# Mixture-of-experts tiles in groups of four, with the narrow down products on two row groups of TensorE

## The reference, cut to what matters

```python
gu = jnp.einsum('th,efh->tef', x, w_gate_up)      # 64 experts, 2 * 176 rows each
g, u = (gu[..., :FFN], gu[..., FFN:])
act = jax.nn.silu(g) * u
act = act * comb[:, :, None]                      # the token's share of expert e
routed = jnp.einsum('tef,ehf->th', act, w_down)   # 176 -> 256
shared = jnp.einsum('tf,hf->th', jax.nn.silu(sg) * su, ws_down)
return routed + shared
```

## Time and profile before

| | |
|---|---|
| median of 3 runs | 294.2 us (292.29 to 294.91) |
| profiled execution | 293.05 us, span 291.2 us |
| TensorE busy | 258.4 us, 89% |
| POOL busy | 178.2 us, 61% |
| DVE busy | 150.3 us, 52% |
| ACT busy | 126.2 us, 43% |
| DMA | 89.08 MB, mean 306 GB/s |

### The profile page before, as it was taken

One profiled execution on the slowest core, in us unless ns is written; L12 is line 12 of the kernel. 1 busy time (PEld: TensorE's weight loads), 2 busy tenths in 40 slices (PEclk: granted clock), 3 DMA queues, 4 the chain that ended last, 5 costly groups with the idle time before them and its releaser, 6 DMA issues.

```text
span 291.2 us, 6600 instructions
## 1 busy us (share of the span) xinstructions
PE 258.4 (89%) x1674; PEld 225.5 (77%) x1674; DVE 150.3 (52%) x696; ACT 126.2 (43%) x374; POOL 178.2 (61%) x155
## 2 busy tenths in 40 slices
PE   6998758888889879999999999999999999999810
PEld 4695436666656669999999999999999999999700
DVE  3834897799996744544433333333333333334355
ACT  2524433332322544555555555555555555555300
POOL 9301257767776734677877667776766665577600
PEclk9999997799999999999999999999999999999995
DMA  6999999999943638999999999999999999988597
GB/s 162 393 429 430 417 361 377 390 399 387 382 173 134 202 85 198 334 327 352 351 353 333 332 321 325 330 325 321 327 323 329 332 332 334 335 184 161 77 322 260
DMA packets 50632, 89.08 MB, mean 306 GB/s; under 512 B 6578, under 2 KB 37379, under 8 KB 49571
## 3 DMA queue, kind: packets, MB, share of 16 engines
q1 hardware_dynamic: 29714, 63.75, 60.9%
q0 software_dynamic: 12816, 17.12, 27.6%
q10 hardware_dynamic: 8064, 7.80, 7.9%
HBM read 58.11 MB, written 30.54 MB: 304 GB/s over the span
## 4 chain that ended last, share of the span: by engine, by line
PE 66%; DVE 17%; DMA 7%; issue 4%; POOL 3%; ACT 2%; SPq 0%; POOLq 0%; DVEq 0%; ACTq 0%
PE PS L1188 29%; PE PS L1200 10%; PE PS L1201 10%; PE PS L1057 5%; PE PS L1140 3%; DVE M L888 2%; DMA VXG<-x_slots 2%; DMA XN<-acc 2%; DVE X L979 2%; POOL x_slots L449 2%; PE PS L1020 2%; DMA acc<-PT,IDR 2%; PE PS L1014 1%; PE PS L1027 1%; PE PS L1035 1%
## 5 line engine op out<-in xcount | busy, mean ns | idle before, releaser
L1188 PEld LDWEIGHTS PS<-XT,WA 128*128 128x128 f32 (+1 forms) x852 | 105.5, 187 | 5.0 <-ACT XNT L556 0.8
L1188 PE MATMUL PS<-XT,WA 128*128 128x128 f32 (+1 forms) x852 | 106.0, 274 | 1.0 <-ACT XNT L556 0.6
L492 POOL DMA_INDIRECT acc<-PT,IDR x52 | 81.0, 1558 | 37.5 <-ACT PT L660 17.3
L934 DVE TENSOR_TENSOR AC<-SG,PS 128x128 f32<-128x128 f32 x71 | 20.4, 288 | 95.6 <-ACT SG L628 95.2
L660 ACT ACTIVATE PT<-PS,WT 128x256 f32<-128x256 f32 x70 | 33.1, 473 | 34.4 <-PE PS L1201 33.7
L446 POOL DMA_INDIRECT x_slots<-HX,SLOT x36 | 35.1, 976 | 16.0 <-issue 9.6
L1200 PE MATMUL PS<-WA,AC 128*128 128x256 f32 x140 | 41.8, 381 | 0.0
L1201 PE MATMUL PS<-WB,AC 128*128 128x256 f32 x140 | 41.7, 379 | 0.0
L492 POOL DMA_INDIRECT out_rows<-PT,IDR x18 | 28.1, 1561 | 14.9 <-ACT PT L660 6.9
L549 ACT COPY XT<-PS 128x256 f32<-128x256 f32 x73 | 27.1, 372 | 19.8 <-PE PS L1057 17.4
L627 ACT ACTIVATE SG<-PS 128x128 f32<-128x128 f32 x71 | 19.7, 277 | 27.8 <-PE PS L1188 27.8
(11 more groups left out here) (154 smaller groups left out, 310.1 us busy)
## 6 DMA issues: line engine op xcount, KB each, us to landing
WA<-in_wa SPq DMA_DIRECT2D x71, 496.0 KB, 13.7
x_slots<-WA SPq DMA_DIRECT2D x1, 8704.0 KB, 28.7
VXG<-x_slots ACTq DMA_DIRECT2D x56, 136.0 KB, 6.6
WB<-in_wb SPq DMA_DIRECT2D x71, 48.0 KB, 16.4
acc<-ZERO SPq DMA_DIRECT2D x2, 1152.0 KB, 18.9
VXG<-x_slots SPq DMA_DIRECT2D x8, 136.0 KB, 2.2
CT<-in_ctxT SPq DMA_DIRECT2D x2, 512.0 KB, 6.1
X<-in_x SPq DMA_DIRECT2D x2, 512.0 KB, 6.2
```

What stands on the lines that cost most here:

```text
L492: pool.indirect_dma_start(acc[j], bass.IndirectOffsetOnAxis(ap=IDR[:, u:u + 1], axis=0), YS[:, u % YR, :], None, compute_op=ALU.add).then_ ...
L934: v.tensor_tensor(AC[:, w % 2, 0, :], SG[:, w % 2, 0, :], PS[:, 4 + w % 2, 0:128], ALU.mult)
L1188: last = mm(PS[0:n, (4 if c == 2 else 2) + w % 2, c % 2 * 128:(c % 2 + 1) * 128], WA[:, base:base + n], XT[:, w % 2, k, :], start=(k == 0) ...
```

## The change

Main tiles go in groups of four (`QUAD = 4`). TensorE does the gate/up products and transposes of four steps, then the four wide down halves, then the four narrow ones. The narrow halves are no longer padded: weights and activations of even tiles lie on partitions 0 to 47, those of odd tiles on 64 to 111, and each product covers just its 48 partitions. `WB` is half as large, and the clears of `WB` and `AC` at the start go, with SP's wait for the first. Only the last of the eight down products signals, with a step of four, so the four results, ACT's copies, POOL's scatters and SP's releases of weight slots come together behind it. Four results live in two PSUM banks, two to a bank, and `AC` holds four wide activations. Late tiles go one by one, with the unpadded narrow half. In the diff the first `quad` is ACT's and the second TensorE's.

```diff
-        AC = sb("AC", [128, 2, 2, 128])
+        AC = sb("AC", [128, QUAD + 2, 128])
-        WB = sb("WB", [128, R * D])
+        WB = sb("WB", [128, R // 2 * D])
...
+        def narrow_weights(u):
+            return WB[UG * (u % 2):UG * (u % 2) + F2, u // 2 * D:(u // 2 + 1) * D]
+        def narrow_rows(w):
+            return AC[UG * (w % 2):UG * (w % 2) + F2, QUAD + w // 2 % 2, :]
+        def result(w):
+            return PS[:, 6 + w % 2, w // 2 % 2 * D:(w // 2 % 2 + 1) * D]
...
-            sp.wait_ge(s_wbz, 1)
...
-            nc.gpsimd.memset(WB[:], 0.0).then_inc(s_wbz, 1)
...
+            def quad(i, u):
+                for j in range(QUAD):
+                    step(i, u + j)
+                for j in range(QUAD):
+                    result_out(i, u + j)
...
-            v.memset(AC[:], 0.0)
...
-                ge(dve, s_d, t + (w - 1))
+                ge(dve, s_d, t + (w - QUAD + 1))
...
+            def wide(i, u, first):
+                pe.wait_ge(s_act, i * U + (u + 1))
+                mm(result(u), AC[:, u % QUAD, :], WA[:, u * WROW + KD * GUW:(u + 1) * WROW], start=first, stop=False,
+                   skip_group_check=not first)
+            def narrow(u, first):
+                return mm(result(u), narrow_rows(u), narrow_weights(u), start=False, stop=True, skip_group_check=not first)
+            def quad(i, u):
+                t = i * U
+                for j in range(QUAD):
+                    gate_up(i, u + j + 1)
+                    rows(i, u + j + LOOK_R)
+                ge(pe, s_y, t + u)
+                for j in range(QUAD):
+                    wide(i, u + j, j < 2)
+                for j in range(QUAD):
+                    last = narrow(u + j, j < 2)
+                last.then_inc(s_d, QUAD)
```

More of the change, by code:

```diff
@@ L47 @@
 X_HELD = 2
+QUAD = 4
 SORTED = B - 2
@@ L201, in program @@
         s_pos = [sem(f"s_pos{p}") for p in range(TOPK)]
-        s_xi, s_xinit, s_wbz = sem("s_xi"), sem("s_xinit"), sem("s_wbz")
+        s_xi, s_xinit = sem("s_xi"), sem("s_xinit")
         s_dve = sem("s_dve")
@@ L320, in load @@
                 sp.dma_start(WA[:, u * WROW:(u + 1) * WROW], big).then_inc(s_w[u % GRP], 16)
-                sp.dma_start(WB[0:F2, u * D:(u + 1) * D], rest).then_inc(s_w[u % GRP], 16)
+                sp.dma_start(narrow_weights(u), rest).then_inc(s_w[u % GRP], 16)
             def load_next(i, u, e):
@@ L641, in step @@
                     x_next(i, w)
-                finish_step(i, u)
+                rows_in(t, u + LOOK_R)
+            def quad(i, u):
[3 more added lines that the diff above has]
+                    result_out(i, u + j)
             def x_next(i, w):
@@ L651, in late_step, with result_out @@
                 silu(i * U, u + 1)
-                finish_step(i, u)
-            def finish_step(i, u):
+                rows_in(i * U, u + LOOK_R)
+                result_out(i, u)
+            def result_out(i, u):
                 t = i * U
-                rows_in(t, u + LOOK_R)
                 act.wait_ge(s_d, t + (u + 1))
@@ L659, in finish_step @@
                 act.wait_ge(s_share, t + (u + 1))
-                nc.scalar.activation(YS[:, u % YR, :], PS[:, 6 + u % 2, 0:D], ACT.Copy,
+                nc.scalar.activation(YS[:, u % YR, :], result(u), ACT.Copy,
                                      scale=WT[:, u % 4:u % 4 + 1]).then_inc(s_y, 1)
@@ L665, in _ @@
             rows_in(0, 2)
-            for u in range(U):
-                step(0, u)
+            for u in range(0, U, QUAD):
+                quad(0, u)
             with act.Fori(1, E // U - 1) as i:
[L669 to L672, removed]
+                for u in range(0, U, QUAD):
+                    quad(i, u)
+            for u in range(0, U, QUAD):
+                quad(E // U - 1, u)
             act.wait_ge(s_list, 1)
@@ L1192, in gate_up, with late_step @@
                 last.then_inc(s_gu, 1)
-            def step(i, u):
+            def wide(i, u, first):
[15 more added lines that the diff above has]
+                last.then_inc(s_d, QUAD)
+            def late_step(i, u):
                 t = i * U
@@ L1197, in step @@
                 rows(i, u + LOOK_R)
[L1198 to L1202, removed]
+                pe.wait_ge(s_y, t + (u - 1))
+                wide(i, u, True)
+                narrow(u, True).then_inc(s_d, 1)
             rows(0, 0)
@@ L1215, in _ @@
             with pe.Fori(1, E // U - 1) as i:
[L1216 to L1220, removed]
+                for u in range(0, U, QUAD):
+                    quad(i, u)
+            for u in range(0, U, QUAD):
+                quad(E // U - 1, u)
+            late_tiles(pe, T, late_step)
             pe.wait_ge(s_xt2, T + LOOK_R)
```

4 lines of the change are left out of this document (2 added, 2 removed).

## The result

The changed kernel takes 299.66 us (median of 4 runs, 297.16 to 301.21), the kernel before 294.56 us (4 runs, 292.29 to 296.05): a ratio of 1.0198, with a 95% interval of 1.0142 to 1.0254. The profiled execution is the one of 297.16 us, with a span of 295.3 us (293.05 and 291.2 before).

A forecast was written before the change was run, and what follows sets the result against it. TensorE was taken as the bound, with 66% of the chain. Span 291.2 - 10.4 + 5.1 + 0.9 + 4.2 + 4.7 = 295.7, with 1.85 around it 297.5; forecast 298 us, range 291 to 304.5.

The forecast's parts named there:

- Narrow passes beside each other: Narrow down halves on TensorE: passes on different rows overlap, five slots for eight per group, -10.4 us over 16 groups.
- Changing the shape: TensorE going to half height and back: 32 changes in the main tiles at 0.16 us each, +5.1 us.
- The start: Tile 0's two down halves now come behind TensorE's wait for tile 4's rows: 2 x 0.43, +0.9 us.
- New waits behind the four results: ACT's four copies in a row may delay a group's second gate/up: nothing to 0.15 us a group, 2.2 in all.
- POOL between tiles 8 and 31: Later scatters there make tile 23's result wait for tile 15's landing; TensorE loses 3.7, then 0.5 us: +4.2.
- Tile 63: End of the last main tile on TensorE: 258.7 us, so the change is worth nothing on TensorE.
- The end: The last group's scatters start only at its end; tile 67's starts 15.9 us after it, for 11.2 before: +4.7 us.
- Behind tile 67's scatter: The chain from tile 67's scatter to the program's end: left alone by the change, 21.1 us as before.

The follow-up runs named there:

- same rows: Changed kernel with all narrow operands on partitions 0 to 47, still grouped and unpadded: 321.82 us, ratio 1.0381 to the kernel before.
- the last kernel above: Changed kernel with its first sixteen tiles in pairs, sixteen result slots and copies shifted by one for tiles below 60: 313.55 us, ratio 0.9947 to the kernel before.
- chip B: Three other chips under one name, kernel before at medians of 309.62, 311.39 and 312.52 us; the unaltered changed kernel has ratios 1.0056 and 1.0035 there.

## Why the prediction was right, point by point

The forecast was 298.0 us, the range 291 to 304.5, and 299.66 was measured; slower by over 1%, which had a chance of 0.60, is what came. By its steps, in the profiled execution:

- **Narrow passes beside each other**, -10.4 us: mis-sized. It took five slots for eight passes; the trace shows four, the lower bound of -13.9. My argument that only b1 could go with a2, and c1 with b2, was wrong: the starts come in pairs of two from the first on. That the cause is the other rows, "same rows" shows.
- **Changing the shape**, +5.1 us at 0.16: measured 0.39 a group, 0.195 a change, so 6.2 in 16 groups. The Trainium skill (TensorEngine Tiling (Array Packing), Key Properties) says that a change of the tiling mode drains the TensorE; the trace agrees that a change has a price, 0.39 us for the way there and back. Both terms together: forecast 9.31 us a group, measured 9.23 undisturbed (with the 0.05 of the second gate/up), so 1.3 us better in 16 groups.
- **The start**, +0.9 us: too small. Tile 3 ended 15.76 us after the first gate/up (115.26 - 99.50), for 14.01 before (114.22 - 100.21), though one group's gain of 0.4 is in it: +2.2. The two moved halves are 0.87 of it, as forecast; 1.6 us are the granted clock behind the longer wait (1.16 on the first gate/up, 0.27 on the second, 0.21 on the transposes), which no step of mine had; and the rows landed 0.2 sooner, counted from the first product.
- **New waits behind the four results**, 0 to 2.2 us, and **POOL between tiles 8 and 31**, +4.2: the 15 groups after the first took 142.49 us (115.26 to 257.75), 4.0 above 15 x 9.23. Of them 2.1 is the wait at the place that was named, tile 23's result near 165 (1.97 at 167.07, forecast 3.7; the landing was earlier than my 9.5 us had it), the rest is up to 0.45 us a group in seven others, at the second gate/up, where the sum had "about even". So +4.0 for +4.2, half of it from the term that I had put at nothing.
- **Tile 63**: forecast 258.7, measured 257.75. "On TensorE the change is worth nothing" holds to 1.2 us.
- **The end**, +4.7 us (15.9 us from tile 63 to tile 67's scatter for 11.2): right in that the results that come out by fours lengthen the tail, too small, and laid to the last group alone. Measured are 17.34 (257.75 to 275.09), so +6.1: not 1.5 us from the group's end to its first scatter but 2.70, as tile 60 waits until tile 57 has landed on its copy (3.32 us idle), and 0.2 of waits within the burst. TensorE's late tiles, 2.80 apart, were covered, as said. In every kernel with a last group of four, G to S67 is 16.5 to 18.1 us, for 11.0 in both traces of the kernel before; with pairs throughout it is 12.8. That holds on every chip. But with only the last group cut in two pairs it is still 17.0 and 17.7: the last group's release and tile 57's landing both hold tile 60's scatter, and they fall within 1.3 us of each other (the scatter starts 2.58 us behind the release here, and 1.27 in the last kernel above, where it waits for no landing). The forecast had only the release. That its term came near is in part luck: the limit that it left out lay close to the one that it had.
- **Behind tile 67's scatter**: 20.2 us for 21.1, forecast without change; tile 69's scatter comes 3.7 behind it instead of 4.75, as POOL no longer waits for TensorE. Span 295.3, forecast 295.7.

The span came out within 0.4 us by luck, as errors of both signs met: groups 1.3 us faster than forecast, start 1.3 slower, waits 0.2 less, the first product 0.7 earlier, the way to tile 67's scatter 1.4 longer, the rest 0.9 shorter. The medians differ by 1.7 us, as the other three runs of the changed kernel took 299.65 to 301.21; in which stretch, no trace shows.

What the experiments add is a bound on the verdict: "slower by over 1%" came on the first chip, while the changed kernel's ratios on two others are 1.0056 and 1.0035, and nothing in the forecast tells the chips apart: that it was the first chip's result is luck too. As far as one trace of each kernel shows, it holds where the kernel before starts its tiles at full clock and with short waits. From the first product to the end the changed kernel is 4.8 us longer in the first two traces (195.8 for 191.0) and 2.2 in those of chip B (197.6 for 195.4), where the kernel before has lost at its start what the change loses on the first chip.

## What to carry to other kernels

Work batched on the engine with the most work hands its results over in bursts. Ask what consumes them, at which fixed pitch, and how far the last one hangs behind: here 0.4 us saved 16 times was paid back once, by 6.1 us in the tail. Where consumers need each other's landings (a copy used in turn), look at which one the first of the last burst waits for before making the burst smaller: two pairs in place of the last four gained nothing here, as the scatter still waited for the landing of a tile of the burst before.

## What was not expected of the hardware

- Two-pass float32 products on rows 0 to 47 and 64 to 111 in turn start two passes at a time, although each product's own two passes use the same rows: 181.52, 181.84, 182.06, 182.27, then the next work at 182.58. Which two go together the records don't say.
- An idle time of 2.03 us on TensorE was followed by 12 passes in 2.49 us instead of 1.33, the lower clock level; one of 1.36 in the same place by none that were slower, and one of 1.97 at 165 us, in the middle of the main loop, by full clock too (167.07 to 168.47, 1.40 us, granted clock 1.00).
- An adding scatter of 128 rows of 1 KB (131 KB) lands in 4.37 us at the end, with the transfer engines at a share of 0.52 (270.14 to 274.50), and holds the next one on its copy back for 8.6 us near the last group (251.86 to 260.45) at a share of 1.08. The Trainium skill (DMA: Bandwidth & Descriptors, Anatomy of one DMA — SWDGE (gpsimd) path) gives a fit by which I estimate 2.3 us; these traces disagree with it for an adding scatter beside other transfers, and none shows one alone.
